# One f32 row and one product in place of three bf16 ones in the maximum rounds of a graph network kernel

## The chip, the cores and the metric

The kernel runs on one core of a Trainium2 chip. The metric is device time in microseconds (us) of one launch; the median of three runs before the change is 7659.45 us (7643.21 to 7665.73). PE is TensorE, PEld its weight loads, DVE is VectorE, ACT is ScalarE, POOL is GpSimd, SP is SyncE; "q" behind a name is that engine's instruction queue issuing a DMA.

## The reference

A graph of 3125 nodes (64 features) and 103125 edges, sorted by destination. Seven rounds over all edges are computed: one normalized sum, two attention convolutions, one sum with a weight matrix by relation, and three maximum convolutions (layer norms stand between the parts). The diff touches the last kind:

```
def _edgeconv(x, src, dst, W1, b1, W2, b2):
    xi = x[dst]
    xj = x[src]
    m = concatenate([xi, xj - xi], axis=-1)
    h = relu(m @ W1 + b1)
    h = h @ W2 + b2
    out = segment_max(h, dst, num_segments=x.shape[0])
    return where(isfinite(out), out, 0.0)
for l in range(3):
    x = relu(_edgeconv(x, src, dst, W1[l], b1[l], W2[l], b2[l]))
```

With W1 split into its halves A and B this is h = relu(x[dst] (A - B) + x[src] B + b1): two tables of 64 values for each node, one read by source and one by destination.

## The kernel before

Edges lie in tiles of 128 and chunks of 512 (TC = 4 tiles). There are 202 chunks. `ROUNDS` names the rounds: SUM, ATT, ATT, REL, MAX, MAX, MAX (numbers 0 to 6). In a MAX round one step takes two chunks, c and c + 101, side by side in the upper and lower 64 partitions, so it has 101 steps. Every engine has its own program; `chunks` lays the parts of a step out with lags (a part with lag 1 works on step c - 1) and `wait` puts the semaphore waits. A buffer is one of U = 4 (in SBUF) or V = 2 (in PSUM).

One step of a MAX round:

- POOL (`gather`, L1086) waits for the indices from ACT and for `turned` of step c - 3, then issues eight indirect DMAs of 128 rows of 64 f32 from the source table into `rows`. SUM and REL rounds issue four for each chunk, ATT rounds four (L1093), so there are 808 in every round. The same queue gathers `agg` (L1114, 25 indirect DMAs of one row a node) at the end of a round.
- SP (`fetch_pair`) waits for `pen_ready` and `turned` of step c - 3, loads the two chunks' one-hots (`sel`, u8 seen as fp8, 128 x 1024), two rows of flags, and four windows of 128 rows of the destination table, which begin at the tile's first node. ACT (`fetch_second`) loads the other chunk's four windows. A destination row is 3 x 64 bf16 (high, middle and low part of the f32 value).
- PE (`turn_pair`, L1319 and L1323) transposes a tile of `rows` into PSUM and adds, for both halves, three products of a 128 x 64 window part (the weights) with the 128 x 128 one-hot (moving): 4 transposes and 24 products a step. Then `lift` (L1398) of step c - 1, an f32 product with W2 over 512 columns, and `back` (L1406) of step c - 2, four transposes.
- ACT: relu with bias (L1227), the penalties from the flags (L1154), `hb` out of PSUM (L1161), and the stores of `hb` into the table of states.
- DVE (`step_plain`, `scan`, L1562): one max scan over 512 columns (`pen` from SBUF, the product from PSUM).

Between rounds stand the node stages (`node_pe`, `node_act`, `node_dve`, `node_stores`), over seven groups of up to four blocks of 128 nodes (the last has one). Their order on each engine is written in `STEPS` and in the `groups` calls. Round 3 (REL) makes the tables for the first MAX round, rounds 4 and 5 those for the next. For a group: DVE joins the gathered rows (and in round 3 the layer norm), PE turns them, ACT copies them out, PE multiplies by `w1` (`pq`, L675: 128 columns, the destination half first), ACT copies the source half out (L645), and the destination half is split in three: ACT `high` (L484), DVE `rest` (L498), ACT `middle` (L490), DVE `low` (L505). SP stores both. In round 3, SP's order is the source rows of group g and then the destination rows of group g - 2 (`groups((0, store_src), (1 if r in (4, 5) else 2, store_dst))`), and `high` of group g waits until the destination rows of group g - 2 are stored:

```
if g >= V:
    act.wait_ge(rounds[q.r + 1].dst_stored[u], 16 * (g // V))
```

The next round's first gather waits for all source stores and for ACT's first indices; ACT issues these after its own wait for both tables (`tables_stored`).

Of the kernel before, what the change touches and what calls it, by code (L numbers as in the profile page):

```python
# [26 lines left out]
P = 128  # L27
TC = 4
EC = TC * P
# [28 lines left out]
def gnn_kernel(nc, src, typ, wgt, dst_row, dst_prev, dst_tile, first, edge_t, x, W, out):  # L58
# [14 lines left out]
    dsts = [dram(f"dst_table{r}", (NT, 3 * w), bf16) if w else None for r, w in enumerate(width)]  # L73
# [7 lines left out]
    with ctx:  # L81
# [15 lines left out]
        zrow = sb("zrow", [P, 3 * KA], bf16)  # L97
# [64 lines left out]
        win_sb = sb("win_sb", [P, U * 2 * TC * 3 * D // 2])  # L162
        win = win_sb[:, :].bitcast(bf16).rearrange("p (u f) -> p u f", u=U)
# [36 lines left out]
        def bank(n, s):  # L200
# [48 lines left out]
            3: dict(dve=[(0, ["added"] + LN1), (3, ["low"]), (1, LN2), (2, ["rest"])],  # L249
                    act=[(0, ["std"]), (2, ["src", "high"]), (1, ["xT"]), (2, ["middle"])],  # L250
# [3 lines left out]
        STEPS[4] = STEPS[5] = dict(dve=[(0, JOIN), (2, ["low"]), (1, ["rest"])],  # L254
                                   act=[(1, ["src", "high"]), (0, ["zT"]), (1, ["middle"])],
# [36 lines left out]
        class Round:  # L292

            def __init__(self, r, kind):
# [17 lines left out]
                if kind == MAX:  # L312
                    self.pen_ready = shared("pen_ready", C_)
                    self.relu_ready = shared("relu_ready", C_)
                    self.lifted = shared("lifted", C_)
# [32 lines left out]
                if kind == MAX:  # L348
                    self.in_ready = [shared(f"in_ready_{s_}", 16 * (2 * TC + 3) * len(range(s_, C_, U))) for s_ in range(U)]
# [105 lines left out]
        def win_pair(s, j, h):  # L455
            return win[:, s, (2 * j + h) * 3 * D:(2 * j + h + 1) * 3 * D]
# [51 lines left out]
        def query_psum(q, g, nb):  # L508

            if q.r in (0, 1):  # L510
                return blocks_of(bank(1 + q.r, g % V), nb, KA)
            return blocks_of(bank(1, g % V), nb, 2 * D)[:, :, 0:D]

        def node_stores(sp, q):
# [10 lines left out]
            def store_dst(g):  # L525
                b, nb = GROUPS[g]
                w = width[r + 1]
                wait(sp, dve_did(q, g, "low"))
# [33 lines left out]
            else:  # L562
                groups((0, store_src), (1 if r in (4, 5) else 2, store_dst))

        def node_act(act, q):
# [69 lines left out]
            def high_out(g):  # L635
                nb = GROUPS[g][1]
                high(act, q, g, nb, width[r + 1], query_psum(q, g, nb), "query" if r < 2 else "pq")
# [4 lines left out]
            def src_high(g):  # L642
                b, nb = GROUPS[g]
                wait(act, pe_did(q, g, "pq"))
                nc.scalar.activation(zn[:, b:b + nb, :], blocks_of(bank(1, g % V), nb, 2 * D)[:, :, D:2 * D], ACT.Copy)\  # L645
# [1076 lines left out]
```

## Time and profile before

| | |
|---|---|
| median of 3 runs (lowest, highest) | 7659.45 us (7643.21, 7665.73) |
| span of the profiled execution | 9918.4 us |
| its own time beside the span | not given; the span runs from the first to the last instruction |
| busy: PE, PEld | 3937.1 us, 2674.1 us |
| busy: DVE, ACT | 2471.0 us, 2035.1 us |
| busy: POOL | 5554.5 us |
| mean granted clock of TensorE | 0.637 of full speed |

Busy time is a union for each engine. The profiled execution took about 2259 us longer than the median run, so times are read from it stretch by stretch and not as a whole. The idle time before an instruction is put down to what released it; "issue" is time in which the engine waited for nothing that the profile shows.

### The profile page before, as it was taken

The page shows a single profiled execution, that of the slowest core. Times are in us where ns is not written, and L with a number is a line of the kernel's source. Part 1 is how long each engine was busy: PE and PEld are TensorE (multiplying, and loading weights), DVE is VectorE, ACT ScalarE, POOL GpSimd, SP SyncE. Part 2 cuts the span into 40 slices and gives each one's busy share as a digit, 9 for nine tenths or more (in the row PEclk, how much of TensorE's full clock was granted, in tenths as well). Part 3 has the DMA queues.
Part 4 walks back from the last instruction along what each step waited for, and adds up shares of the span by engine and source line. Part 5 has one row for each costly group of instructions (what it writes and reads, how often), then busy time and mean ns, then how long its engine had stood idle before and what let it go on. Part 6 is the DMA issues. An engine that isn't in the chain of part 4 may idle for free.

```text
span 9918.4 us, 123616 instructions
## 1 busy us (share of the span) xinstructions
PE 3937.1 (40%) x24024; PEld 2674.1 (27%) x24024; DVE 2471.0 (25%) x4351; ACT 2035.1 (21%) x6406; POOL 5554.5 (56%) x5874
## 2 busy tenths in 40 slices
PE   2333334443343433336222224444444444444443
PEld 1222223333342333334111112222222222222222
DVE  4333333333332333332222221111111111111112
ACT  1111123333332333333101111111111111111111
POOL 6666644454434444442666665666656666556665
PEclk9999995555555555555555555666656666566666
DMA  4444434454444444443222223333333333333333
GB/s 121 126 126 126 125 91 108 109 110 107 108 92 97 109 106 107 107 107 99 54 50 50 51 48 82 91 90 90 89 79 90 90 90 90 80 89 90 91 91 80
DMA packets 2188624, 925.94 MB, mean 93 GB/s; under 512 B 1608302, under 2 KB 2071734, under 8 KB 2182134
## 3 DMA queue, kind: packets, MB, share of 16 engines
q1 hardware_dynamic: 1080022, 458.65, 19.0%
q10 hardware_dynamic: 921120, 272.38, 11.7%
q0 software_dynamic: 187392, 193.93, 9.6%
q8 instruction: 30, 0.49, 0.0%
q14 instruction: 60, 0.49, 0.0%
HBM read 657.48 MB, written 266.58 MB: 93 GB/s over the span
## 4 chain that ended last, share of the span: by engine, by line
issue 30%; PE 20%; another core or an unknown queue 9%; SPq 7%; DVE 2%; DVEq 1%; ACT 1%; DMA 0%; ACTq 0%; POOL 0%; POOLq 0%
PE ps L1323 7%; PE ps L1398 5%; PE ps L1319 3%; SPq L1002 3%; PE ps L1406 2%; PE ps L675 1%; PE ps L1309 1%; DVEq L374 1%; SPq L996 1%; SPq L1004 1%; SPq L998 1%; DVE edges_a L1580 1%; DVE st L1562 0%; SPq L370 0%
## 5 line engine op out<-in xcount | busy, mean ns | idle before, releaser
L1086 POOL DMA_INDIRECT edges_a<-src_table,idx x4040 | 3829.6, 948 | 2501.2 <-issue 1163.6
L1093 POOL DMA_INDIRECT edges_a<-src_table,idx x1616 | 1524.7, 944 | 1626.7 <-ACT weighted L1209 1063.1
L1323 PE MATMUL ps<-sel,win_sb 128*64 128x128 fp8e4 x7272 | 749.7, 262 | 1704.9 <-issue 1703.6
L1562 DVE TENSOR_TENSOR_SCAN st<-pen,st,ps 128x512 f32<-128x512 f32 x300 | 384.0, 1280 | 3279.9 <-remote 2939.6
L1406 PE MATMUL ps<-ident,st 64*128 64x64 f32 (+2 forms) x4444 | 849.1, 339 | 655.0 <-DVE st L1562 333.8
L1406 PEld LDWEIGHTS ps<-ident,st 64*128 64x128 f32 (+2 forms) x4444 | 705.6, 207 | 1063.1 <-issue 1039.8
L1323 PEld LDWEIGHTS ps<-sel,win_sb 128*64 128x64 bf16 x7272 | 396.2, 126 | 2056.6 <-issue 2009.9
L1562 DVE TENSOR_TENSOR_SCAN st<-edges_a,st,ps 64x512 f32<-64x512 fp8e4 x402 | 510.5, 1270 | 1665.6 <-remote 1292.0
L1309 PE MATMUL ps<-ident,edges_a 128*64 128x128 f32 x1616 | 421.4, 416 | 985.2 <-DVE edges_a L1580 643.5
L1335 PE MATMUL ps<-win_sb,sel 128*128 128x97 bf16 x4848 | 473.8, 271 | 849.1 <-issue 771.5
L1163 ACT ACTIVATE hb<-ps 128x256 f32<-128x256 f32 (+1 forms) x808 | 348.4, 431 | 2000.1 <-remote 1082.1
L1390 PE MATMUL ps<-ident,weighted 128*97 128x128 f32 x1616 | 452.8, 433 | 615.9 <-issue 279.9
L1595 DVE TENSOR_TENSOR prod<-ps,edges_a 128x388 f32<-128x388 f32 x404 | 225.4, 558 | 1795.3 <-remote 1459.7
L1335 PEld LDWEIGHTS ps<-win_sb,sel 128*128 128x128 fp8e4 x4848 | 396.1, 135 | 909.9 <-issue 826.0
L1319 PE MATMUL ps<-ident,edges_a 128*128 128x128 f32 x1212 | 439.2, 362 | 425.3 <-issue 354.7
L1227 ACT ACTIVATE edges_a<-ps,b 128x512 f32<-128x512 f32 x303 | 208.2, 687 | 1658.0 <-remote 1498.9
L1390 PEld LDWEIGHTS ps<-ident,weighted 128*97 128x97 f32 x1616 | 337.5, 274 | 659.9 <-issue 640.2
L1562 DVE TENSOR_TENSOR_SCAN st<-decay,st,ps 97x512 f32<-97x512 f32 x402 | 511.5, 1272 | 10.4 <-PE ps L1406 10.4
L1309 PEld LDWEIGHTS ps<-ident,edges_a 128*64 128x64 f32 x1616 | 216.4, 158 | 1063.7 <-issue 996.2
L1161 ACT ACTIVATE hb<-ps 128x512 f32<-128x512 f32 x303 | 180.9, 597 | 1555.4 <-issue 1386.1
L1398 PE MATMUL ps<-edges_a,w 128*128 128x512 f32 x606 | 481.9, 887 | 9.7 <-issue 8.0
L1209 ACT ACTIVATE weighted<-edges_a,weight 128x97 f32<-128x97 f32 x1616 | 471.9, 364 | 33.3 <-ACT hb L1163 23.9
(203 smaller groups left out, 3440.4 us busy)
## 6 DMA issues: line engine op xcount, KB each, us to landing
states_sum<-hb ACTq DMA_DIRECT2D x1010, 128.0 KB
win_sb<-dst_table SPq DMA_DIRECT2D x1616, 72.8 KB
edges_a<-src_table,idx POOLq DMA_INDIRECT x5656
states_att<-hb ACTq DMA_DIRECT2D x404, 194.0 KB
win_sb<-dst_table ACTq DMA_DIRECT2D x1212, 48.0 KB
win_sb<-dst_table SPq DMA_DIRECT2D x1212, 48.0 KB
dst_b<-in_dst_row SPq DMA_DIRECT2D x50, 1024.0 KB
sel<-onehots SPq DMA_DIRECT2D x303, 128.0 KB
```

The lines of the kernel that those rows point to most:

```text
L1086: pool.indirect_dma_start(rows[:, s, j * D:(j + 1) * D], None, srcs[q.r], bass.IndirectOffsetOnAxis(ap=idx[:, s, j:j + 1], axis=0))\
L1093: pool.indirect_dma_start(xe_a[:, s, j * KA:j * KA + D], None, srcs[q.r], bass.IndirectOffsetOnAxis(ap=idx_a[:, s, j:j + 1], axis=0))\
L1163: nc.scalar.activation(hb[:, v, 0:TC * kw], bank(BACK, s)[:, 0:TC * kw], ACT.Copy)\
L1209: last = nc.scalar.activation(weighted[:, s % V, j * KA:(j + 1) * KA], xe_a[:, s, j * KA:(j + 1) * KA], ACT.Copy, scale=weight[:, gs_, o + ...
L1309: last = nc.tensor.matmul(bank(TURNED, s)[0:D, j * P:(j + 1) * P], rows[:, s, j * D:(j + 1) * D], ident[:, :], is_transpose=True, start=Tr ...
L1319: nc.tensor.matmul(bank(TURNED, s)[:, at_j], rows[:, s, j * P:(j + 1) * P], ident[:, :], is_transpose=True, start=True, stop=False)
L1323: last = nc.tensor.matmul(bank(TURNED, s)[h * D:h * D + D, at_j], win_pair(s, j, h)[:, i * D:(i + 1) * D], sel[:, s, h * EC + j * P:h * EC ...
L1335: last = nc.tensor.matmul(bank(TURNED, s)[:, j * KA:(j + 1) * KA], sel[:, v, j * P:(j + 1) * P], win_att(v, j)[:, i * KA:(i + 1) * KA], st ...
L1390: last = nc.tensor.matmul(bank(QUERY, s)[0:KA, j * P:(j + 1) * P], weighted[:, s % V, j * KA:(j + 1) * KA], ident[:, :], is_transpose=True ...
L1398: nc.tensor.matmul(bank(QUERY, s), w2[:, q.r - 4, :], xe[:, s, :], start=True, stop=True).then_inc(q.lifted.sem, 1)
L1406: last = nc.tensor.matmul(bank(BACK, s)[:, j * w:(j + 1) * w], st[0:w, s % V, j * P:(j + 1) * P], ident[0:w, 0:w], is_transpose=True, star ...
L1562: nc.vector.tensor_tensor_scan(st[0:w, s % V, :], d0, d1, init, op0, op1).then_inc(q.st_ready.sem, 1)
```

## The change

In the three MAX rounds the destination table holds one f32 row of 64 values for a node. `turn_pair` makes one f32 product for each tile and half, where it made three of bf16. Its moving operand must be f32 too, so DVE copies the one-hots of a step (128 x 1024) from fp8 to f32 (`widen`), into memory that only the SUM round used (`dst_b`). In the node stages of rounds 3, 4 and 5 `high`, `rest`, `middle` and `low` become one ACT copy, `dst`, and SP stores the destination rows of group g right after its source rows in all three. `turn_pair` has a new wait for `sel_wide`; on DVE `widen` of step c stands ahead of the scan of step c - 1. SP waits for `turned` only ahead of the windows, not ahead of the one-hots.

```
-    dsts = [dram(f"dst_table{r}", (NT, 3 * w), bf16) if w else None for r, w in enumerate(width)]
+    dsts = [dram(f"dst_table{r}", (NT, D), f32) if k == MAX else dram(f"dst_table{r}", (NT, 3 * KA), bf16) if k == ATT
+            else None for r, k in enumerate(ROUNDS)]
...
+        sel_f = dst_b[:, :, :].rearrange("p u e -> p (u e)").bitcast(f32).rearrange("p (u e) -> p u e", u=U)
...
-            3: dict(dve=[(0, ["added"] + LN1), (3, ["low"]), (1, LN2), (2, ["rest"])],
-                    act=[(0, ["std"]), (2, ["src", "high"]), (1, ["xT"]), (2, ["middle"])],
+            3: dict(dve=[(0, ["added"] + LN1), (1, LN2)],
+                    act=[(0, ["std"]), (2, ["src", "dst"]), (1, ["xT"])],
...
-        STEPS[4] = STEPS[5] = dict(dve=[(0, JOIN), (2, ["low"]), (1, ["rest"])],
-                                   act=[(1, ["src", "high"]), (0, ["zT"]), (1, ["middle"])],
+        STEPS[4] = STEPS[5] = dict(dve=[(0, JOIN)], act=[(1, ["src", "dst"]), (0, ["zT"])],
...
         def win_pair(s, j, h):
-            return win[:, s, (2 * j + h) * 3 * D:(2 * j + h + 1) * 3 * D]
+            return win_f[:, s, (2 * j + h) * D:(2 * j + h + 1) * D]
...
+                if nxt.kind == MAX:
+                    wait(sp, act_did(q, g, "dst"))
+                    sp.dma_start(dsts[r + 1][b * P:(b + nb) * P, :].rearrange("(b p) f -> p b f", p=P), dst_rows_out(g))\
+                        .then_inc(nxt.dst_stored[g % V], 16)
+                    return
...
-                groups((0, store_src), (1 if r in (4, 5) else 2, store_dst))
+                groups((0, store_src), (0 if r > 2 else 2, store_dst))
...
-                high_out(g)
+                if g >= V:
+                    act.wait_ge(rounds[r + 1].dst_stored[g % V], 16 * (g // V))
+                nc.scalar.activation(dst_rows_out(g), pq[:, :, 0:D], ACT.Copy).then_inc(q.act.sem, 1)
...
             def pq(g):
-                    wait(pe, dve_did(q, g - V, "rest"), act_did(q, g - V, "high"))
+                    wait(pe, act_did(q, g - V, "dst"))
...
                 def fetch_pair(c, s, n):
-                    wait(sp, (q.pen_ready, c - U + 1), (q.turned, c - U + 1))
+                    wait(sp, (q.pen_ready, c - U + 1), (q.sel_wide, c - U + 1))
...
+                    wait(sp, (q.turned, c - U + 1))
                     fetch_windows(sp, q, c, s, 0)
...
                 def turn_pair(c, s, n):
+                         (q.sel_wide, c + 1), (q.relu_ready, c - V + 1))
...
-                            for i in range(3):
-                                last = nc.tensor.matmul(bank(TURNED, s)[h * D:h * D + D, at_j],
-                                                        win_pair(s, j, h)[:, i * D:(i + 1) * D],
-                                                        sel[:, s, h * EC + j * P:h * EC + (j + 1) * P],
-                                                        start=False, stop=i == 2)
+                            last = nc.tensor.matmul(bank(TURNED, s)[h * D:h * D + D, at_j], win_pair(s, j, h),
+                                                    sel_f[:, s, h * EC + j * P:h * EC + (j + 1) * P],
+                                                    start=False, stop=True)
...
+                def widen(c, s, n):
+                    wait(dve, (q.sel_ready[s], 16 * (n + 1)), (q.turned, c - U + 1))
+                    nc.vector.tensor_copy(sel_f[:, s, :], sel[:, s, 0:2 * EC]).then_inc(q.sel_wide.sem, 1)
...
+                elif k == MAX:
+                    chunks(dve, q.steps, (0, widen), (1, step_plain))
```

## Rows read from the trace of the kernel before

**Rows 1.** The page: busy time by engine.

```profile
PE 3937.1 (40%) x24024; PEld 2674.1 (27%) x24024; DVE 2471.0 (25%) x4351; ACT 2035.1 (21%) x6406; POOL 5554.5 (56%) x5874
```

**Rows 2.** Stretches of the seven rounds' gathers: length, busy (count) by engine, clock, DMA.

```profile
1344.00:2879.00 1535.00, 603.66 (x4306) 519.77 (x4307) 552.34 (x1010) 501.69 (x1812) 762.47 (x808) 0.57 0.49 108
...
7295.00:8539.00 1244.00, 540.26 (x3334) 293.86 (x3334) 122.81 (x96) 183.95 (x389) 762.05 (x808) 0.63 0.38 89
...
sum 9201.00, PE 3608.43 PEld 2437.62 DVE 2198.71 ACT 1858.02 POOL 5352.92; mean PE 515.49 PEld 348.23 DVE 314.10 ACT 265.43 POOL 764.70
```

**Rows 3.** Timeline of POOL in a MAX round: the first and last of 13 gathers.

```profile
7608.07 0.94 POOL L1086 DMA_INDIRECT edges_a<-src_table,idx  x1 [0.30 <-issue]
...
7623.04 0.94 POOL L1086 DMA_INDIRECT edges_a<-src_table,idx  x1 [0.30 <-issue]
```

**Rows 4.** The same round: POOL by groups of instructions, then a row of its waits.

```profile
L1086 POOL DMA_INDIRECT edges_a<-src_table,idx x808 | 762.2, 943 | 499.0 <-issue 233.0 <-PE ps L1323 230.0 <-ACT idx L1146 36.0
...
PE ps L1323 <- issue: 549.5, 386, 3.2
```

**Rows 5.** PE at either clock: two short stretches, and the timeline of `lift` and `pq`.

```profile
7246.00:7249.00 3.00, 3.00 (x29) 1.84 (x28) 0.75 (x1) 1.47 (x3) 0.00 (x0) 1.00 0.39 87
...
7282.00:7284.00 2.00, 1.73 (x8) 1.73 (x8) 1.86 (x6) 0.64 (x2) 0.00 (x0) 0.50 0.70 168
...
7238.91 2.08 PE L1398 MATMUL ps<-edges_a,w 128*128 128x512 f32 x2
...
7244.07 1.12 PE L1398 MATMUL ps<-edges_a,w 128*128 128x512 f32 x2
...
7247.62 1.13 PE L1398 MATMUL ps<-edges_a,w 128*128 128x512 f32 x2
...
7282.27 2.07 PE L675 MATMUL ps<-w,hT 64*128 64x128 f32 x8 [1.13 <-ACT hT L571]
```

**Rows 6.** DVE by groups: a converting copy before round 0; the scan of a MAX round.

```profile
L1473 DVE CAST rel_i<-mask 128x808 int32<-128x808 f32 x1 | 0.6, 582 | 0.0
...
L1562 DVE TENSOR_TENSOR_SCAN st<-pen,st,ps 128x512 f32<-128x512 f32 x95 | 121.6, 1280 | 1056.5 <-remote 941.3 <-PE ps L1398 63.2 <-issue 33.5
```

**Rows 7.** Timeline at the start of SUM, then POOL and DVE groups of that round.

```profile
64.13 1.56 POOL L1086 DMA_INDIRECT edges_a<-src_table,idx  x1 [16.14 <-DMA src_table<-zn]
64.60 1.17 DVE L1538 TENSOR_SCALAR rel_rows<-rel_rows 128x1542 f32<-128x1542 f32 x2
...
68.85 1.95 POOL L1086 DMA_INDIRECT edges_a<-src_table,idx  x1 [0.31 <-issue]
69.68 0.99 DVE L1550 TENSOR_SCALAR row_pen<-row_pen 1x1616 f32<-1x1616 f32 x1
...
L1086 POOL DMA_INDIRECT edges_a<-src_table,idx x808 | 773.0, 957 | 452.3 <-issue 237.3 <-remote 146.0 <-ACT idx L1150 52.6
...
L1569 DVE TENSOR_SCALAR sel<-dst_b,nodes 128x128 fp8e4<-128x128 int32 x796 | 176.7, 298 | 6.3 <-DMA edges_a<-flags 6.3
```

**Rows 8.** Timeline of the node stage of round 3.

```profile
5933.76 1.06 PE L668 MATMUL ps<-ident,xn 128*64 128x128 f32 x4 [4.82 <-issue]
...
5936.56 0.94 POOL L1114 DMA_INDIRECT agg<-states_sum,last_i  x1 [0.30 <-issue]
...
5963.24 0.51 SPq L529 DMA_DIRECT2D dst_table<-split  x1
5965.65 0.38 ACT L484 ACTIVATE split<-ps 128x256 bf16<-128x256 f32 x1 [2.85 <-DMA dst_table<-split]
...
5969.49 0.51 SPq L529 DMA_DIRECT2D dst_table<-split  x1
...
5980.01 0.94 POOL L1086 DMA_INDIRECT edges_a<-src_table,idx  x1 [42.51 <-ACT idx L1146]
```

**Rows 9.** Timeline of the end of the node stage of round 4.

```profile
7288.99 0.79 PE L675 MATMUL ps<-w,hT 64*128 64x128 f32 x2 [0.55 <-ACT hT L571]
...
7294.97 0.94 POOL L1086 DMA_INDIRECT edges_a<-src_table,idx  x1 [17.03 <-ACT idx L1146]
```

More of the change, by code:

```diff
@@ L96, in gnn_kernel @@
         eps = sb("eps", [P, 1])
-        zrow = sb("zrow", [P, 3 * KA], bf16)
+        zrow = sb("zrow", [P, 3 * KA + 1], bf16)
         wq = [sb(f"wq{l}", [D + 1, D]) for l in range(2)]
@@ L314, in __init__ @@
                     self.relu_ready = shared("relu_ready", C_)
+                    self.sel_wide = shared("sel_wide", C_)
+                    self.sel_ready = [shared(f"sel_ready_{s_}", 16 * len(range(s_, C_, U))) for s_ in range(U)]
                     self.lifted = shared("lifted", C_)
@@ L348, in __init__ @@
                 if kind == MAX:
-                    self.in_ready = [shared(f"in_ready_{s_}", 16 * (2 * TC + 3) * len(range(s_, C_, U))) for s_ in range(U)]
+                    self.in_ready = [shared(f"in_ready_{s_}", 16 * (2 * TC + 2) * len(range(s_, C_, U))) for s_ in range(U)]
                 uses = [(C_ - s_ + U - 1) // U for s_ in range(U)]
@@ L655, in node_act @@
             elif r == 3:
-                groups((0, std), (2, src_high), (1, xT_out), (2, middle_out))
+                groups((0, std), (2, src_dst), (1, xT_out))
             elif r in (4, 5):
-                groups((1, src_high), (0, zT_out), (1, middle_out))
+                groups((1, src_dst), (0, zT_out))
             else:
@@ L872, in node_dve @@
             elif r == 3:
-                groups((0, related), (3, low_of), (1, normed), (2, rest_of))
+                groups((0, related), (1, normed))
             elif r in (4, 5):
-                groups((0, joined), (2, low_of), (1, rest_of))
+                groups((0, joined))
             else:
@@ L933, in _ @@
                 if width[r]:
-                    sp.dma_start(dsts[r][NP:NT, :], zrow[:, 0:3 * width[r]]).then_inc(zeros_stored, 16)
+                    zeros = zrow[:, :].bitcast(f32)[:, 0:D] if rounds[r].kind == MAX else zrow[:, 0:3 * KA]
+                    sp.dma_start(dsts[r][NP:NT, :], zeros)\
+                        .then_inc(zeros_stored, 16)
             sp.wait_ge(flags_made, 2)
@@ L1152, in penalty @@
                 def penalty(c, s, n):
-                    wait(act, (q.in_ready[s], 16 * (2 * TC + 3) * (n + 1)), (q.st_ready, c - V + 1))
+                    wait(act, (q.in_ready[s], 16 * (2 * TC + 2) * (n + 1)), (q.st_ready, c - V + 1))
                     nc.scalar.activation(pen[:, s % V, :], sel[:, s, 2 * EC:], ACT.Copy, scale=BIG, bias=-BIG)\
@@ L1662, in _ @@
                            (1, running), ring=UA)
+                elif k == MAX:
+                    chunks(dve, q.steps, (0, widen), (1, step_plain))
                 else:
-                    chunks(dve, q.steps, (0, step_plain), ring=U if k == MAX else 2 * U)
+                    chunks(dve, q.steps, (0, step_plain), ring=2 * U)
                 if k == MAX:
```

20 lines of the change are left out of this document (10 added, 10 removed).

## The prediction

> **What bounds the kernel now.** I read the page first, then a table by stretches, POOL's timeline, POOL's groups and waits. The page's share of busy time misleads here: POOL is busy 5554.5 us of 9918.4 [rows 1], yet the profiled execution, by its span, is 2259 us longer than the median run of 7659.45 us, so first it must be said which of its times the unprofiled run has. The seven stretches in which POOL gathers edge rows last 9201 us together [rows 2], with 7 x 808 = 5656 gathers. In a MAX round 12 gathers begin in 7623.04 - 7608.07 = 14.97 us, one each 1.248 us [rows 3]: 0.943 us busy and 0.30 us to the next. At that pitch 5656 gathers need 7059 us, so POOL stood still for 9201 - 7059 = 2142 us more. The stretches' excess is nearly the whole difference between the two executions (2142 of 2259). For one MAX round: 1244 us against 808 x 1.248 = 1008, so 236 us excess, and that is the 230 us in which POOL waits for PE's L1323 [rows 4]. PE in turn stands for 549.5 us on "issue" ahead of L1323 [rows 4], a wait for nothing in the kernel, though at full clock it does a whole step in 7247.62 - 7244.07 = 3.55 us [rows 5]. The ATT stretch has 4306 PE records in 1535 us, the MAX stretch 3334 in 1244 us [rows 2]: 2.8 and 2.7 records in each us, with quite different work. So I take PE's stalls as an effect of recording, and the unprofiled run as one in which POOL gathers without a break in all rounds: 9.98 us for each MAX step of eight gathers, against some 3.6 to 7 us of PE. What PE gains or loses inside that is worth nothing; what delays a gather, or the start of the next round's gathers, is paid in full.
>
> **PE's part.** Each tile and half has three bf16 products now and one f32 product afterwards. An f32 product shows as two records: `lift` has two for each product, and the eight records of `pq` are four products with 128 columns [rows 5]. These eight took 2.07 us at clock 0.50 (the 1.2 GHz level), or 0.26 us a record with the first load. A step gets 8 products, 16 records: 2 x 2.07 = 4.1 us, and its four transposes about 0.8 us (an estimate from the 29 records in 3.00 us at full clock [rows 5]: 0.1 us each, twice that here), so `turn_pair` is some 4.9 us at the low level and half of it at full clock. The whole PE step is then 4.9 + 2.1 (`lift` [rows 5]) + 0.8 (`back`, four transposes again) = 7.8 us at the low level. Cost: nothing, behind 9.98 us of gathers; if that cover were gone, up to 1 us a step (24 bf16 records in place of these 16 took less).
>
> **The widening copy.** A converting copy of 808 columns took 582 ns [rows 6], L1550 with 1616 columns 0.99 us [rows 7]; the slope is (0.99 - 0.58) / 808 = 0.5 ns a column, so 1024 columns take about 0.69 us. As time of DVE it is free: DVE has 122.8 us of work in 1244 us [rows 2]. It adds a serial chain, though: on DVE `widen` of c is queued behind the scan of c - 2, which waits for `lift` of c - 2, which PE does after `turn_pair` of c - 1; and `turn_pair` of c waits for `widen` of c. The loop is 4.9 + 2.1 + 1.28 (scan [rows 6]) + 0.69 + about 0.4 for four hops = 9.4 us at the low clock, under 9.98. Cost zero, with 0.6 us of margin; behind `widen` stands only the scan, for which `back` and ACT wait, with two steps of room.
>
> What it does to POOL is the term that decides. At the start of SUM two long DVE operations with one SBUF input ran beside gathers [rows 7]. The gather of 64.13 took 1.56 us in place of 0.94 and ended at 65.69, 0.12 us after the first of L1538's two (0.97 of the row's 1.17 us, to 65.57). The one of 68.85 took 1.95 us and ended at 70.80, 0.13 us after L1550 (70.67). So a gather that comes to its end while such an operation runs is held until this is over. In MAX rounds today the 808 gathers have a mean of 943 ns, none held [rows 4]; in SUM the mean is 957 ns beside 796 short operations of L1569 [rows 7]. For a copy of length h at a random place in the pitch of 1.248 us, one point that must not be covered costs h x h / (2 x 1.248) a step: 0.19 us at h = 0.69. Two such points (start and end of a gather) cost up to 0.38. From below: in SUM 773.0 - 762.2 = 10.8 us of 202 chunks, 0.054 us for four short ones; scaled with the square of the length (4 x 0.21 squared = 0.18, 0.69 squared = 0.48) this is 0.15 us. The largest possible is a full block in each step, 0.69 + 0.12 = 0.81 us. A reason for less than zero there is none; zero would be a copy that always falls between the points. I take 0.28 us, between 0.15 and 0.38 since the two long operations are nearer in form than the short ones: 303 steps x 0.28 = +85 us. Bounds 0 and 303 x 0.81 = +245 us.
>
> The Trainium skill ("SBUF — State Buffer", "Who interferes with whom") says that a DVE copy or cast in a 2-port mode holds the port pair it shares with GpSimd for its whole length, the other side being blocked until it ends plus about 115 ns; the trace agrees (0.12 and 0.13 us [rows 7]). It speaks against this change: by it each copy that meets a gather's descriptor writing costs up to its full length.
>
> **The node stages.** In round 3 the stores of destination rows go out each 5969.49 - 5963.24 = 6.25 us, and `high` waits 2.85 us until the store just issued has landed (5963.24 to 5965.65) [rows 8]. The reason is SP's order: the rows of group g - 2 leave after the source rows of g, hence after `pq` of g. Afterwards this wait goes, since group g - 2 is stored two groups earlier. Late next is the loop PE `pq` 2.07 + turn about 1.1 + ACT's copy about 0.6 = 3.8 us, and above that POOL itself, four `agg` gathers for each group, 4 x 1.25 = 5.0 us. In the profile POOL's last `agg` gather starts at 5936.56 and the first of the next round at 5980.01, 43.5 us later. Behind that gather I count 1.5 (landing) + 2.3 + 0.6 + 1.5 + 0.7 (DVE for groups 5 and 6) + 1.1 + 0.6 + 2.1 + 0.4 + 0.3 + 0.8 (PE and ACT) + 0.5 + 2.9 (copies, store) + 1.0 = 16.3 us (estimates of the order of the rows' durations), so 27 us less in the profiled execution. The unprofiled run gains less: in the profile this stage's first turn stood until 5933.76 behind PE's stalls [rows 8], almost at POOL's last gather, and all the 6.25 us loops came after it; without stalls the loops run beside POOL's 5.0 us a group, and seven of them save 7 x 1.25 = 9 us. With the shorter tail I take 11 us, bounds 5 and 27. In rounds 4 and 5 only the tail shortens: from the last `pq` to the first gather it is now 7294.97 - 7288.99 = 6.0 us [rows 9], of which `rest`, `middle`, `low` and their hops are about 1.5 us: 2 x 1.5 = 3 us, bounds 0 and 6. Together -14 us. The changed SP order moves one wait behind three DMA issues, which only lets them go earlier: nothing. The smaller rows (256 B for 384) take load off the DMA engines, busy 0.38 [rows 2]: nothing. The last step of a round has up to 1 us more of PE ahead of its states, beside the first twelve `agg` gathers (15 us): 0, at most +3.
>
> **Sum.** In the profiled execution: 9918 - 27 - 3 + 85, and 3 x 236 = 708 us of recording stalls fall away where 26 records a step (34 now) at 2.7 in a us need 9.6 us, less than POOL's 10.3: about 9265 us of span. For the unprofiled time, which has no such stalls, the terms stand on the median: 7659 - 14 + 85 = 7730 us. A difference of 0.3%, 23 us, is what a measurement of this kernel can tell from none.
>
> **Rivals.** (1) The copy costs POOL nothing, because it runs in a form that doesn't hold POOL or falls between: 7659 - 14 = 7645 us, at most 7626 with the full node gain. For it: L1562's scans beside gathers in MAX rounds delay none today. Against it: L1538 and L1550 are of the copy's form. (2) Full block in every step, since the copy is timed by PE's and POOL's own rhythm and may always meet the same point: 7659 - 14 + 245 = 7890 us; at a half of it, 7767. (3) The loop over PE and DVE is longer than 9.98 us, that is from 0.6 us over my count on, for instance when POOL also holds the copy back (L1569 took 298 ns in the mean for 128 columns) and the clock stays at the low level: with 10.6 us, 303 x 0.6 = +188, 7833 us. (4) PE's "issue" stalls exist without the profiler too: 34 records to 26 would then free 708 us of POOL's waits, 7659 - 14 + 85 - 708 = 7022 us. Against it stands the sum above: 2142 us of stalls can't be in a run that is 2259 us shorter.
>
> **How the numbers follow.** My forecast of a partial hold, 20 to 180 us, has 0.68; (1) 0.17, (2) 0.07, (3) 0.05, (4) 0.03. Predicted: 7730 us. The range takes in most of (1) and the forecast up to 0.6 us a step (7659 - 14 + 182 = 7827): 7640 to 7830. Faster by over 23 us: (4) and the part of (1) with a large node gain, 0.12. Within 23 us: the rest of (1) and a hold below 0.12 us a step, 0.20. Slower: 0.68.
>
> **What would show it.** In the changed kernel's profile: MAX stretches near 808 x 1.248 + 28 = 1040 us with hardly a POOL wait for PE; gathers beside a DVE copy of about 0.69 us with durations of 1.0 to 1.6 us, and a mean over the MAX rounds near 943 + 35 = 978 ns; 16 product records a step; in round 3 no ACT wait for a destination store, and about 16 us from the last `agg` gather to the next round; span about 9265 us. The prediction is wrong if gathers keep a mean of 944 ns (then rival 1), if POOL waits for PE or DVE with the MAX steps over 10.5 us (rival 3), or if the copy takes over 1.1 us.

## The result and the profile after

The changed kernel takes 7695.91 us (7694.63 to 7699.88, 4 runs) against 7659.11 us (7643.21 to 7665.73, 4 runs) of the kernel before: ratio 1.0047, interval 1.0035 to 1.0059, 36.8 us slower. Run again later beside other kernels it was 7694.53 against 7655.12, ratio 1.0052 (1.0039 to 1.0066).

The page of the kernel after, span 7692.8 us; busy time by engine, answering to [rows 1]:

```profile
PE 4136.4 (54%) x21600; PEld 2601.8 (34%) x21600; DVE 2685.0 (35%) x4612; ACT 2010.9 (26%) x6385; POOL 5615.5 (73%) x5874
```

The first profile of the kernel before ("before" from here on; "after" is the changed kernel) had a span of 9918.4 us. A second one of the same kernel (`b_again`, below) has 7644.6, like its timed runs, and is the one to compare with. Its stretches of gathers (round 3, then the three MAX rounds; length, busy and count of PE, PEld, DVE, ACT, POOL, granted clock, DMA share, GB/s):

```profile
3395.00:4405.00 1010.00, 331.41 (x1604) 207.95 (x1604) 341.37 (x402) 117.24 (x398) 764.05 (x808) 0.50 0.27 59
4466.00:5474.00 1008.00, 623.63 (x3390) 322.75 (x3390) 126.61 (x99) 189.04 (x398) 761.92 (x808) 0.59 0.49 111
5526.00:6534.00 1008.00, 623.81 (x3390) 322.71 (x3390) 126.60 (x99) 189.03 (x398) 761.93 (x808) 0.59 0.49 111
6586.00:7594.00 1008.00, 621.89 (x3390) 321.31 (x3390) 126.61 (x99) 189.02 (x398) 761.98 (x808) 0.60 0.49 111
```

The same stretches of the kernel after, answering to [rows 2]:

```profile
3397.00:4410.00 1013.00, 331.12 (x1604) 207.61 (x1604) 341.36 (x402) 117.65 (x398) 766.92 (x808) 0.50 0.28 58
4459.00:5484.00 1025.00, 682.14 (x2590) 320.93 (x2590) 191.71 (x200) 189.19 (x398) 778.91 (x808) 0.58 0.43 96
5534.00:6562.00 1028.00, 680.22 (x2590) 320.29 (x2590) 190.72 (x200) 189.18 (x398) 781.65 (x808) 0.59 0.43 95
6613.00:7641.00 1028.00, 679.70 (x2590) 319.85 (x2590) 189.26 (x200) 189.19 (x398) 781.51 (x808) 0.59 0.43 95
```

The MAX stretches are 17, 20 and 20 us longer: 57 us together, or 0.19 us in each of 303 steps. POOL's own busy time grew by as much (2342.1 against 2285.8 us), so no wait was added: gathers became longer. PE is busy 58 us more in a round, at the same clock, and the step doesn't get longer by it (experiment 1). The gaps between rounds went the other way. From the end of a round's last edge gather to the first of the next (gather rows of both traces) they were 60.9, 51.3 and 51.9 us and are 48.9, 49.8 and 50.9: 14.5 us less. 57 - 14.5 = 42 us, of which the timed runs show 37 to 39. The trace of the second comparison (`a_again`) has 51 us more in the stretches and 17.4 less in the gaps, 34 together. Of the 57, some 6 stand in this one trace alone: there every gather, beside a copy or not, is 3 ns longer (median 947 ns; 944 in `a_again` and `b_again`). The gap behind round 2, which the change does not touch, varies from 148 to 162 us from trace to trace, so whole spans tell less than stretches do.

The groups of POOL and of DVE's copy in the first MAX round of after [rows 4, 6]:

```profile
L1102 POOL DMA_INDIRECT edges_a<-src_table,idx x808 | 779.3, 965 | 262.8 <-issue 242.1 <-ACT idx L1162 16.7 <-PE ps L1338 3.7
...
L1607 DVE CAST dst_b<-sel 128x1024 f32<-128x1024 fp8e4 x101 | 73.5, 728 | 14.9 <-DMA sel<-onehots 14.9
```

And the timeline of two steps in the second MAX round, answering to [rows 3, 5] (start, duration, idle before):

```profile
5801.04 0.45 PE L1335 MATMUL ps<-ident,edges_a 128*128 128x128 f32 x1 [3.76 <-DMA edges_a<-src_table,idx]
...
5801.42 0.69 PE L1338 MATMUL ps<-dst_b,win_sb 128*64 128x128 f32 x4
...
5805.13 2.03 PE L1412 MATMUL ps<-edges_a,w 128*128 128x512 f32 x2
...
5807.45 1.28 DVE L1576 TENSOR_TENSOR_SCAN st<-pen,st,ps 128x512 f32<-128x512 f32 x1 [8.48 <-issue]
5808.14 1.29 POOL L1102 DMA_INDIRECT edges_a<-src_table,idx  x1 [0.30 <-issue]
5808.64 0.67 DVE L1607 CAST dst_b<-sel 128x1024 f32<-128x1024 fp8e4 x1
5809.73 0.94 POOL L1102 DMA_INDIRECT edges_a<-src_table,idx  x1 [0.30 <-issue]
...
5811.51 0.44 PE L1335 MATMUL ps<-ident,edges_a 128*128 128x128 f32 x1 [3.92 <-DMA edges_a<-src_table,idx]
...
5818.48 0.94 POOL L1102 DMA_INDIRECT edges_a<-src_table,idx  x1 [0.30 <-issue]
5819.15 0.79 DVE L1607 CAST dst_b<-sel 128x1024 f32<-128x1024 fp8e4 x1
5819.73 1.02 POOL L1102 DMA_INDIRECT edges_a<-src_table,idx  x1 [0.30 <-issue]
```

`turn_pair` takes 5805.13 - 5801.04 = 4.1 us, and PE then stands 3.9 us waiting for rows. The gather of 5808.14, beside a copy from 5808.64 to 5809.31, ends at 5809.43 in place of 5809.08: 0.12 us behind the copy. The next copy differs: it begins late in a gather (5819.15, 0.67 us behind the start at 5818.48), is itself long (0.79 us), and the next gather loses 0.08 us.

### The profile page after: what moved, and what is told of

Read it like the earlier page. It is cut to its first block, busy times and chain, and to the rows that moved or that the text cites. A ratio compares the mean times of both kernels' runs of the same rounds, so it can differ in the third digit from the quotient of the medians.

```text
span 7692.8 us, 119855 instructions
## 1 busy us (share of the span) xinstructions
PE 4136.4 (54%) x21600; PEld 2601.8 (34%) x21600; DVE 2685.0 (35%) x4612; ACT 2010.9 (26%) x6385; POOL 5615.5 (73%) x5874
## 4 chain that ended last, share of the span: by engine, by line
POOL 33%; issue 16%; PE 5%; DMA 5%; DVE 1%; ACT 1%; POOLq 1%; ACTq 0%; DVEq 0%; SPq 0%
POOL edges_a L1102 31%; DMA edges_a<-src_table,idx 5%; PE ps L1338 1%; POOL edges_a L1109 1%; PE ps L1335 1%; PE ps L1325 1%; PE ps L688 1%; POOL agg L1130 1%; PE ps L783 0%; DVE st L1576 0%; PE ps L1404 0%; DVE edges_a L1594 0%; POOLq L378 0%; PE ps L1420 0%; POOLq L1123 0%
## 5 line engine op out<-in xcount | busy, mean ns | idle before, releaser
L1102 POOL DMA_INDIRECT edges_a<-src_table,idx x4040 | 3883.8, 961 | 1396.1 <-issue 1168.6
L1109 POOL DMA_INDIRECT edges_a<-src_table,idx x1616 | 1529.5, 946 | 534.9 <-issue 443.2
L1335 PE MATMUL ps<-ident,edges_a 128*128 128x128 f32 x1212 | 556.8, 459 | 1060.3 <-DMA edges_a<-src_table,idx 1060.3
L1338 PE MATMUL ps<-dst_b,win_sb 128*64 128x128 f32 x4848 | 829.6, 441 | 0.0
L1335 PEld LDWEIGHTS ps<-ident,edges_a 128*128 128x128 f32 x1212 | 217.4, 179 | 1454.2 <-issue 1302.3
L1412 PE MATMUL ps<-edges_a,w 128*128 128x512 f32 x606 | 624.6, 1134 | 0.0
L1404 PE MATMUL ps<-ident,weighted 128*97 128x128 f32 x1616 | 388.7, 383 | 307.0 <-ACT weighted L1225 166.5
L1338 PEld LDWEIGHTS ps<-dst_b,win_sb 128*64 128x64 f32 x4848 | 353.9, 203 | 263.3 <-issue 254.2
L1349 PE MATMUL ps<-win_sb,sel 128*128 128x97 bf16 x4848 | 408.3, 256 | 41.8 <-DMA win_sb<-dst_table 41.8
L1404 PEld LDWEIGHTS ps<-ident,weighted 128*97 128x97 f32 x1616 | 286.5, 237 | 351.4 <-issue 332.2
L1349 PEld LDWEIGHTS ps<-win_sb,sel 128*128 128x128 fp8e4 x4848 | 366.1, 127 | 52.0 <-DMA win_sb<-dst_table 44.0
```

What stands on the lines that cost most here:

```text
L1102: pool.indirect_dma_start(rows[:, s, j * D:(j + 1) * D], None, srcs[q.r], bass.IndirectOffsetOnAxis(ap=idx[:, s, j:j + 1], axis=0))\
L1109: pool.indirect_dma_start(xe_a[:, s, j * KA:j * KA + D], None, srcs[q.r], bass.IndirectOffsetOnAxis(ap=idx_a[:, s, j:j + 1], axis=0))\
L1335: nc.tensor.matmul(bank(TURNED, s)[:, at_j], rows[:, s, j * P:(j + 1) * P], ident[:, :], is_transpose=True, start=True, stop=False)
L1338: last = nc.tensor.matmul(bank(TURNED, s)[h * D:h * D + D, at_j], win_pair(s, j, h), sel_f[:, s, h * EC + j * P:h * EC + (j + 1) * P], sta ...
L1349: last = nc.tensor.matmul(bank(TURNED, s)[:, j * KA:(j + 1) * KA], sel[:, v, j * P:(j + 1) * P], win_att(v, j)[:, i * KA:(i + 1) * KA], st ...
L1404: last = nc.tensor.matmul(bank(QUERY, s)[0:KA, j * P:(j + 1) * P], weighted[:, s % V, j * KA:(j + 1) * KA], ident[:, :], is_transpose=True ...
```

## Experiments

Times are medians beside runs of the kernel before on the same chip.

**1. No copy** (`a_no_copy`). The products multiply what lies in the buffer; PE waits for the fp8 one-hots in place of the copy, and SP waits for `turned` ahead of the one-hots again, as in before.

```
-                    chunks(dve, q.steps, (0, widen), (1, step_plain))
+                    chunks(dve, q.steps, (1, step_plain))
```

> This is the kernel after without VectorE's widening copy: the f32 one-hots are never written, so the products multiply what lies in that buffer; every transfer, product and node stage stays. Theory (the copy holds up POOL's gathers, the rest of the change gains in the node stages): the three Maximum rounds' gather stretches fall from 1025, 1028 and 1028 us to the 1011 to 1013 us that the Attention and Relational rounds have, some 50 us together, and the time falls from 7696 to about 7646 us, 13 below before. Rival one (the copy costs nothing, the f32 products or the later transfers cost the 37 us): the time stays near 7696 and the stretches near 1027. Rival two (the copy costs exactly the 37 us and the node stages gain nothing): 7659.

7642.03 us against 7655.95: ratio 0.998 (0.9971 to 0.9989). The theory's time within 4 us, and the stretches are those of before, with the f32 products in them; of the first MAX round:

```profile
4468.00:5476.00 1008.00, 677.26 (x2590) 318.99 (x2590) 126.54 (x99) 189.16 (x398) 761.92 (x808) 0.59 0.44 97
```

So the whole loss hangs on the copy, and the rest of the change gains 14 us. PE's f32 products cost nothing here, which rules out rival one.

**2. The copy on ScalarE** (`a_copy_act`).

```
+                    nc.scalar.activation(sel_f[:, s, :], sel[:, s, 0:2 * EC], ACT.Copy).then_inc(q.sel_wide.sem, 1)
...
-                    chunks(act, q.steps, (U, features), (0, indices), (U, penalty), (0, fetch_second),
+                    chunks(act, q.steps, (U, features), (0, indices), (U, penalty), (0, fetch_second), (2, widen),
```

> The kernel after with the widening copy made by ScalarE (in its stream behind the window fetches, two steps late) in place of VectorE. The output is the same. Theory (what costs is VectorE's copy beside POOL's gathers, not the copy as a step of the chain from one-hots to products): about 7646 us, as without a copy, and Maximum stretches of about 1012 us. Rival one (the copy costs as a link of the chain, or its memory traffic does, whichever engine makes it): 7690 to 7700. Rival two (ScalarE, with some 0.9 us more in a step, becomes late with indices and states): above 7700.

7639.72 us against 7655.95: ratio 0.9983 (0.9974 to 0.9992). It is the copy's engine that costs, not that a copy is made. ScalarE's copy takes longer, and no gather beside it does:

```profile
L1258 ACT ACTIVATE dst_b<-sel 128x1024 f32<-128x1024 fp8e4 x101 | 106.7, 1056 | 174.2 <-issue 174.2
...
L1102 POOL DMA_INDIRECT edges_a<-src_table,idx x808 | 762.3, 943 | 262.2 <-issue 242.7 <-ACT idx L1162 17.4 <-PE ps L1342 2.1
```

**3. The copy twice** (`a_copy_twice`), the second behind the first's semaphore.

```
+                    nc.vector.tensor_copy(sel_f[:, s, :], sel[:, s, 0:2 * EC]).then_inc(q.sel_once.sem, 1)
+                    wait(dve, (q.sel_once, c + 1))
```

> The kernel after with the widening copy made twice, the second behind the first on VectorE. Theory (each copy holds up POOL by some 0.16 us in each of 303 steps): another 50 us, 7746 us, the stretches at about 1042 us and the mean gather some 16 ns longer again. Rival one (the copy costs nothing to POOL; the products or transfers cost): near 7696. Rival two (the serial loop of PE and VectorE sets the pace: 0.8 us more in each step): 303 x 0.8 = 240 us more, about 7940.

7747.20 us against 7655.95: 91 us over before, 53 over after. The stretches are 1049, 1049 and 1040 us: 113 over before's, for the 51 to 57 of one copy. POOL's group in the first MAX round:

```profile
L1103 POOL DMA_INDIRECT edges_a<-src_table,idx x808 | 802.7, 993 | 262.6 <-issue 244.2 <-ACT idx L1163 16.6 <-PE ps L1339 1.8
```

**4. The kernel before with the copy alone** (`b_plus_copy`): `widen` and its semaphores in the kernel before, into a buffer that no product reads.

> The kernel before with one part of the change alone: VectorE widens the one-hots of each step to f32 in a buffer that no product reads, and PE waits for it as in the kernel after; three bf16 products, bf16 destination rows and the old node stages stay. Theory (the copy alone is the cost): 7659 + 50 = 7709 us. Rival one (f32 products, f32 windows or their order cost the 37 us): near 7659. Rival two (the copy costs 37 us and there is no gain elsewhere): 7696.

7697.18 us against 7655.95: ratio 1.0055 (1.0042 to 1.0069), 41 us, under the 50 expected and near rival two's number. The stretches say why: 1022.5, 1024.1 and 1019.0 us, 40 over before's. The copy is the same; it meets the gathers at other points, 174 of the 303 in the first 0.3 us of a gather, where it costs least (35 in after; the table below). Rival two's number is met by chance: its reason (the copy costs 37 us in after and the rest gains nothing) is refuted by experiment 1, which shows the gain. POOL's group in the first MAX round:

```profile
L1089 POOL DMA_INDIRECT edges_a<-src_table,idx x808 | 776.5, 961 | 275.0 <-issue 244.7 <-ACT idx L1149 29.0 <-PE ps L1326 1.2
```

**5. The copy through PSUM** (`a_copy_psum`): on VectorE still, as a maximum with a bank of zeros.

```
-                    nc.vector.tensor_copy(sel_f[:, s, :], sel[:, s, 0:2 * EC]).then_inc(q.sel_wide.sem, 1)
+                    two = lambda a: a.rearrange("p (h e) -> p h e", h=2)
+                    nc.vector.tensor_tensor(two(sel_f[:, s, :]), two(sel[:, s, 0:2 * EC]),
+                                            ps[:, 5, :].unsqueeze(1).to_broadcast([P, 2, EC]), ALU.max)\
+                        .then_inc(q.sel_wide.sem, 1)
```

> The kernel after with the widening made on VectorE still, in the same place, but as a maximum of the one-hots with a bank of zeros in PSUM: one operand is no longer in SBUF, and the instruction should take about 1.2 us in place of 0.73. Same output. Theory (what holds up POOL is a shared way into SBUF that the fast copy takes, not VectorE's time or the chain): the gathers are free again, stretches of about 1010 us, the time about 7645 us although VectorE works some 0.5 us longer in each step. Rival one (any instruction of VectorE beside a gather holds it in proportion to its time): 50 x 1.2 / 0.73 = 82 us over 7642, 7725 us. Rival two (the chain of PE and VectorE is now the pace, 9.9 us and more): above 7700, with POOL's gathers evenly late, 9.98 us turned to over 10.2 a step.

7634.27 us against 7649.59: ratio 0.998 (0.9971 to 0.9989). VectorE needs 1.2 us instead of 0.7 for the same values, and the kernel is 1 part in 150 faster than after (by the ratios 0.998 and 1.0047). Groups of the first MAX round:

```profile
L1609 DVE TENSOR_TENSOR dst_b<-sel,ps 128x1024 f32<-128x1024 fp8e4 x101 | 120.8, 1196 | 14.0 <-DMA sel<-onehots 14.0
...
L1103 POOL DMA_INDIRECT edges_a<-src_table,idx x808 | 762.4, 944 | 262.6 <-issue 243.6 <-ACT idx L1163 16.9 <-PE ps L1339 2.1
```

Rival two is out too: a chain 0.5 us longer still fits in POOL's 9.98 us. The instruction differs from the copy in two things at once, one operand in PSUM and two inputs in place of one, so the runs don't say which of the two frees POOL. The Trainium skill ("SBUF — State Buffer", "Who interferes with whom") says that an instruction of VectorE with at most one SBUF input, outside its 2-port modes, doesn't contend with GpSimd; the runs agree (944 ns a gather against 965).

**6. Products twice** (`a_products_twice`): each f32 product issued twice, the destination part added twice.

```
-                        for h in range(2):
+                        for i, h in enumerate((0, 1, 0, 1)):
```

> The kernel after with each of PE's f32 products issued twice (the destination part is added twice, so the values differ): 16 products in a step in place of 8. By the kernel after, a tile of a transpose and two products takes about 1.03 us at PE's lower clock; two products more make it about 1.7 us and the step's part some 7 us in place of 4.1. Theory (PE's work on the products is covered by POOL's 9.98 us a step): 7696 to 7705 us. Rival one (the products' time is a part of the 37 us, or becomes it): each step 2.8 us longer, of which as much shows as PE is on the path; PE's own step would be 4.1 + 2.8 + 2.0 + 1.7, some 10.6 us, 303 x 0.6 = 180 us more, about 7880. Rival two (a busier PE gets a higher clock): at or below 7696 with a granted clock above 0.66.

7699.59 us against 7649.59: ratio 1.0067 (1.0051 to 1.0082). That is 3.7 us over after by the medians, and 15 by the ratios, whose intervals overlap; the stretches are 1030.4, 1031.5 and 1029.6 us, 10 over after's. Of the first one:

```profile
4455.00:5485.00 1030.00, 724.56 (x4190) 427.99 (x4190) 185.37 (x199) 188.53 (x397) 783.93 (x808) 0.70 0.43 95
```

Doubled products cost under a tenth of rival one's 180 us. But the load was less than planned: PE got a clock of 0.70 in place of 0.58 with them, so `turn_pair` took 4.8 us in the steps looked at, for the 7 expected and 4.1 in after, and PE was busy only 42 us more in the round. So a step of PE above POOL's 9.98 us was never tried. That PE's products don't cost is carried by experiment 1, not by this one. The higher clock is rival two's sign but not its time: since POOL sets the pace, the clock is worth nothing. The 10 us aren't PE's time either: POOL's busy time grew by 10 of them, because the copy falls at another point of the gathers.

**7. The old order of the stores** (`act_old_order`), in the kernel of experiment 2.

```
-                groups((0, store_src), (0 if r > 2 else 2, store_dst))
+                groups((0, store_src), (1 if r in (4, 5) else 2, store_dst))
```

> The kernel with ScalarE's widening copy, and SyncE's stores of destination rows put back to where the kernel before has them: two groups behind the source rows at the end of round 3, one group behind in rounds 4 and 5. Theory (the 14 us of the node stages come from the operations removed from VectorE and ScalarE, and the order of the stores adds little): 7640 to 7645 us. Rival (the earlier stores are what brings it): all 14 us come back, 7654, with 61 us between the rounds 3 and 4 in place of 48.

7646.04 us against 7649.59: ratio 0.9992 (0.9983 to 1.0001), beside experiment 2's 0.9983. The intervals overlap, so the times alone don't decide; the traces do. The theory fell: the gap behind round 3 is 58.2 us again (60.9 in before, 48.0 in experiment 2), behind rounds 4 and 5 it is 50.2 (49.0 and 49.1). So 10 of the 13 us that experiment 2 gains behind round 3 come from the order of the stores, and the removed operations bring the rest. The waits at the end of round 3 in this kernel, and POOL's in experiment 2:

```profile
ACT split_r L660 <- DMA dst_table<-split_r: 13.3, 5, 2.9
...
POOL edges_a L1102 <- ACT idx L1162: 26.2, 1, 26.2
```

```profile
POOL edges_a L1102 <- ACT idx L1162: 16.1, 1, 16.1
```

ScalarE waits five times, up to 2.9 us, for the store of the buffer that it writes again.

**8. The kernel before again** (`b_again`).

> The kernel before once more, unchanged, for a profile whose recording does not hold PE up (its first one has a span of 9918 us against runs of 7659). Theory: a span near 7655 us, Maximum stretches of 1008 to 1013 us, and 61, 51 and 51 us between the last gather of rounds 3, 4 and 5 and the first of the next (as in the kernel before with the copy alone), against 48 to 49 in the kernels with f32 rows. Rival (the gathers of the kernel before are held up in Maximum rounds too, by its 24 products in a step or the scan): stretches above 1015 us. If it is stretched by the recording again, it tells nothing of either.

7646.38 us, span 7644.6; the theory's numbers throughout (stretches above). No MAX gather of before is held. Its waits at the end of round 3, answering to [rows 8]:

```profile
ACT split L484 <- DMA dst_table<-split: 14.4, 5, 3.2
...
POOL edges_a L1086 <- ACT idx L1146: 28.7, 1, 28.7
```

The kernel after has 16.7 us there, and no such wait of ScalarE:

```profile
POOL edges_a L1102 <- ACT idx L1162: 16.7, 1, 16.7
```

**9. The kernel before with the new order of stores** (`b_new_order`): experiment 7's line the other way round.

> The kernel before with one line of the change alone: at the end of round 3, and of rounds 4 and 5, SyncE stores each group's destination rows right behind its source rows, in place of two groups (one group) later. The three bf16 parts and their operations stay. In the last profile of before, ScalarE stands at the end of round 3 five times, 14.4 us in all, for the store of the split buffer that it is to write again. Theory (what the change gained at the end of round 3 is mostly this order): these waits go, the stretch between the last gather of round 3 and the first of round 4 falls from 61 to about 51 us, the time by about 10 us against before. Rival one (in the kernel before the bf16 parts of a group are finished so late that SyncE, waiting for them, sends the next source rows late): no gain or up to 15 us slower, with SyncE's waits on the last part in place of ScalarE's. Rival two (the operations on the parts are as long as the waits): within 3 us of before.

9894.16 us (11 runs) against 9915.31 (9901.3 to 9935.43, 15 runs of before): ratio 0.9982 (0.9973 to 0.9992). On this chip the kernel before takes 2260 us more as well. The gain is 18 us by the ratio (8 to 27), so rival two (within 3 us) is out, and so is rival one. Against the first profile of before, whose span is like these runs, the gap behind round 3 is 64.6 us for 77.5, and ScalarE's 14 us of waits for the store are gone. The order alone is worth 13 us there. On a chip without the 2260 us this kernel wasn't run. POOL's wait behind round 3 in the first profile, and here:

```profile
POOL edges_a L1086 <- ACT idx L1146: 42.5, 1, 42.5
...
POOL edges_a L1086 <- ACT idx L1146: 29.1, 1, 29.1
```

**10. The copy in four pieces** (`a_copy_split`, `a_copy_split2`).

```
-                    nc.vector.tensor_copy(sel_f[:, s, :], sel[:, s, 0:2 * EC]).then_inc(q.sel_wide.sem, 1)
+                    for i in range(4):
+                        last = nc.vector.tensor_copy(sel_f[:, s, i * EC // 2:(i + 1) * EC // 2],
+                                                     sel[:, s, i * EC // 2:(i + 1) * EC // 2])
+                    last.then_inc(q.sel_wide.sem, 1)
```

> The kernel after with VectorE's copy of 1024 columns made as four copies of 256 columns back to back. In the kernel after a gather that has begun under 0.55 us before the copy ends up 0.12 us behind the copy's end, and one that would begin beside the copy's tail is held as well, 0.17 us a step in the mean. Theory (POOL gets its turn only between two instructions of VectorE): with four short ones it gets in between them, a gather waits for a quarter of the copy at most, and the 54 us that the copy costs fall to some 20 to 30 us: 7665 to 7675. Rival (POOL gets no turn in between pieces that follow without a gap, or each piece costs a hold of its own): 7696 or more, since four copies take about 0.2 us more than one.

On the chip of experiment 9: 9963.06 us against 9915.31, ratio 1.0055 (1.0042 to 1.0069). The theory's gain isn't there. The MAX stretches are 1261, 1265 and 1264 us against 1243, 1244 and 1239 of the first profile of before, of which POOL's longer gathers are only 12 us; the rest are waits. What the pieces do to the gathers is seen on a chip without the 2260 us, beside the kernel after:

> The kernel after, unchanged, beside the next kernel on the same chip: 7696 us or 0.47% above before if this chip runs PE as the chip of the first comparison did. On the chip of the last two kernels every program stands some 2250 us longer in stalls that the profile puts at PE's issue, before too (9915 us); if such a chip comes again, the ratio shows what the change costs there. Theory of the held gathers: the copy is beside gathers there too, but 758 of 807 pitches are not stretched by stalls, so the loss stays at 40 to 60 us less the 16 us of the node stages. Rival (on such a chip the f32 products or the link through VectorE lengthen a loop that is then the pace): 60 us and more.

7694.53 us against 7655.12, ratio 1.0052, on a chip without the stalls. What the change as made costs on the other one stays unmeasured.

> The kernel after with VectorE's copy made as four of 256 columns, once more, beside the kernel after on the same chip. In its last trace, in the steps in which no stall of PE fell, four copies of about 0.28 us took 0.92 us together, and a gather beside them was held 77 ns a step in place of 175 for the one long copy. Theory (POOL gets its turn between two pieces): 303 x 0.10 = 30 us below the kernel after, about 7666 us on a chip where after takes 7696. Rival (the pieces hold POOL as long as one copy, and what the last trace shows is the choice of steps): equal to the kernel after or above it.

7658.93 us, ratio 1.0005 (0.9996 to 1.0014): 36 us under after on the same chip, where 30 were expected. The MAX stretches are 33 us shorter than `a_again`'s. Groups of the first MAX round, and two gathers beside pieces:

```profile
L1608 DVE CAST dst_b<-sel 128x256 f32<-128x256 fp8e4 x402 | 97.7, 304 | 14.7 <-DMA sel<-onehots 14.7
...
L1102 POOL DMA_INDIRECT edges_a<-src_table,idx x808 | 768.1, 951 | 262.6 <-issue 241.5 <-ACT idx L1162 17.2 <-PE ps L1338 4.0
```

```profile
4718.02 0.94 POOL L1102 DMA_INDIRECT edges_a<-src_table,idx  x1 [0.31 <-issue]
...
4718.57 1.11 DVE L1608 CAST dst_b<-sel 128x256 f32<-128x256 fp8e4 x4
...
4719.27 1.02 POOL L1102 DMA_INDIRECT edges_a<-src_table,idx  x1 [0.30 <-issue]
```

The pieces run across the end of the first gather and the start of the second; the first isn't held, the second loses 0.08 us. Over all steps, sorted like the table further down, pieces that begin 0.4 to 0.5 us into a gather cost POOL 81 ns, where the long copy costs 299, and those that begin over 1.0 us in about 64 for 422; the mean is 59 ns a step for the 169 of `a_again`. VectorE works longer, POOL goes through in between.

## Why the prediction came out as it did

The forecast (7730, "slower") had sign and mechanism right and was 34 us too high; 7696 lies in the range. By its steps:

**POOL without a break in every round: right. Why the first profile was longer: wrong.** In the second profile of before the MAX stretches are 1008 us, the 808 x 1.248 of the prediction. But the 2142 us of stalls were not an effect of recording: executions recorded on other chips have none (`b_again`: span 7644.6), and on one chip all 15 timed runs of before took 9901 to 9935 us, as long as the first profile. The argument that stalls can't be in a run that is 2259 us shorter was sound; the step to "recording" wasn't. The chip of the first profile isn't on record; that it was one like this is likely, not shown. What the stalls come from is open; the profile puts them at "issue" and "remote".

With that step fell the span of 9265 us (measured 7692.8). The reasoning in it, and in rival 4, that fewer PE records free time from the stalls has a run against it too: `a_copy_split` has the 26 records a step on the chip with the stalls, and its MAX stretches are 63 us longer than before's 34 records took, where 708 less were expected; its gap behind round 3 is 10 us shorter, where 27 were. In its first MAX round PE waits for the four-piece copy (30 times, up to 11.4 us), and the same kernel elsewhere not at all in that round.

```profile
PE ps L1335 <- DVE dst_b L1608: 210.1, 30, 11.4
```

**PE's part costs nothing: right.** `turn_pair` is 4.1 us for a predicted 4.9, and the product records are 16 a step (experiment 6, which issues each product once more, has 4848 more records in its 303 steps). With the f32 products and no copy the stretches are before's 1008 us.

**The copy's time and the serial loop: right.** 0.73 us in the first MAX round (0.69 predicted; 0.67 where nothing delays it), and the loop had room for 0.5 us more (experiment 5). That the products need the copy at all (an f32 table with the fp8 one-hots as they are) was not tried in any run.

**The hold of POOL: the term that was mis-sized, +85 us predicted, 51 to 57 measured** (after less no copy: 1.0047 - 0.998 of 7656 is 51; the stretches 51 and 57). The gathers' mean is 965 to 968 ns for 978, the longest takes 1.45 us (1.0 to 1.6 predicted). The mechanism was shown three ways: take the copy away, double it, and make it by another engine or another instruction. The size was the choice of 0.28 us a step, in the middle between one point that must not be covered (0.19) and two (0.38). Of the 303 copies of the kernel after, 299 (the others stand beside a longer pause), sorted by when they begin after the start of the gather they fall in, show which (excess is what this gather and the next then take over 1.248 us, summed, in ns):

```
begins (us)   0.0-0.2  0.2-0.3  0.3-0.4  0.4-0.5  0.5-0.6  0.6-0.8  0.8-0.9  0.9-1.0  over 1.0
copies             18       17       43       40       45       93       19        6        18
excess (ns)        12      104      198      299      213       80      140      249       422
```

The change from one case to the other is sharp, at 0.545 us into the gather. A copy that begins before that and is still running near the gather's end (about 0.12 us ahead of it) holds it to its own end + 0.12 us, as predicted. One that begins between 0.55 and 0.8 us waits itself (0.77 us long in the mean beyond 0.6, in place of 0.67) and holds the next gather by 0.08; the column from 0.5 to 0.6 mixes both cases (365 and 80 ns). One that begins later covers the next gather's start and holds that. Spread evenly over the pitch this table gives 0.20 us, close to the one-point value of 0.19. That is luck: there are two points, as the prediction feared, but about 0.07 us of the 0.20 come from the gather's end and 0.13 from the next one's start, and the first is small because the copy gives way in part of the cases. As the copies fall it is 0.17 in after and in `a_again`, 0.13 in `b_plus_copy` and 0.22 in `a_products_twice`, and that is why their stretches are 51 to 57, 40 and 66 us over before's for the same copy. The lower bound (0.15, scaled from SUM's short operations) was nearer than the value taken, but it isn't a firm one: it takes 0.21 us for each of L1569's operations, and with their mean of 298 ns [rows 7] it would be 0.07. The prediction left out that the copy gives way too, when the gather is there first; that takes the long tail off.

**The node stages: right, -14 us predicted, 14.5 measured in the trace of after** (round 3: 12.0 for 11; rounds 4 and 5: 2.5 for 3), 15.5 to 18 in the other traces with f32 rows on chips without the stalls. The cause named, SP's order, is shown by experiments 7 and 9 for 10 and 13 us behind round 3. The tail from the last `agg` gather to the next round is 17.6 us for 16.3.

Rival 1 (7645 us) is what the kernel takes once the copy is gone or moved: 7634 to 7642. Rivals 2 and 3 didn't come (in rival 3's line 303 x 0.6 is 182, not 188; its 7833 belongs to 0.62 us).

Two versions are faster than both kernels: the f32 rows with ScalarE's copy (ratio 0.9983) or with the copy through PSUM (0.998), some 0.65% ahead of the change as made. Against before they gain 0.2%, about the node stages' share. That is less than the 0.3% that the prediction called measurable, but the intervals of their 11 runs lie below 1. Experiment 9 has as large a ratio (0.9982) with one line, though on the chip with the stalls alone.

## What to carry to other kernels

Where, as here, GpSimd issues indirect DMAs back to back and sets the pace, a copy or cast on VectorE was paid for in GpSimd's time, not VectorE's. Three ways out worked: the copy on ScalarE, the same values by a two-input instruction with one operand in PSUM (1.6 times as long), or, on a chip without the stalls, the copy in four pieces. The price of one copy was 0.13 to 0.22 us a step, by phase alone; no formula for it was tested beyond this case. A store's place in a queue is read by who waits for its buffer, and before a profile longer than its timed runs is put down to the profiler, the kernel is run on another chip.

## What was not expected of the hardware

- The same program took 7650 to 7659 us (medians) on the other chips and 9915 us on one. In the first profile, which has the same length, POOL's gathers take the same 943 ns, one each 1.248 us where none waits, and the rest are pauses; PE's granted clock in the MAX stretches was 0.63 for 0.59.
- Four casts of 256 columns, back to back, took 0.98 us in the mean (0.87 to 1.13) against 0.67 for an undisturbed one of 1024, and cost the kernel 36 us less.
- A copy that began up to 0.545 us after a gather's start ran at full length and held the gather; one that began from then on was itself delayed, up to 0.91 us long, and the gather ended on time.
- In the Maximum stretches PE's granted clock rose from 0.58 to 0.70 with twice the products, on the same 10 us steps.
